# Setup moved into the first loop steps, and the residual's h added by an identity matmul

## The reference, cut to what matters

```python
h = layernorm(x) * (1 + ca) + sa
x = x + ga * attn(h)            # attn(h) = h + h_out @ W_out.T
h = layernorm(x) * (1 + cb) + sb
x = x + gb * ffn(h)             # 8 experts, top 4 of 8, clipped SwiGLU
```

## Time and profile before

| | us |
|---|---|
| median of 3 runs (lowest to highest) | 864.83 (863.77 to 866.02) |
| the profiled execution | 862.44 |
| its span, first to last instruction | 860.7 |
| what lies around the span | 1.7 |

### The profile page before, as it was taken

The page is one execution under the profiler, slowest core; times in us unless marked ns, Lnnn a source line. Parts: engine busy times, 40 slices in busy tenths (PEclk is TensorE's granted clock), DMA queues, the critical chain, the costliest instruction groups (busy, mean ns, idle before and its releaser), DMA issues.

```text
span 860.7 us, 11466 instructions
## 1 busy us (share of the span) xinstructions
PE 621.6 (72%) x2762; PEld 460.0 (53%) x2762; DVE 708.6 (82%) x1833; ACT 545.1 (63%) x1267; POOL 686.7 (80%) x731
## 2 busy tenths in 40 slices
PE   4743404597878787777869787877779695868886
PEld 3411102375666556555647556555646474757775
DVE  3452999999898998989998999989998999998431
ACT  3444323566767776768676776767676767556785
POOL 0498868798988998999988998989998888734454
PEclk9877756698897989999997999999979899789999
DMA  8008375555364546373553635553736455640000
GB/s 236 10 4 198 76 157 116 119 113 109 81 132 85 111 88 146 70 161 73 131 103 80 131 75 112 103 127 73 161 65 142 86 130 97 140 88 7 14 6 7
DMA packets 90659, 85.28 MB, mean 99 GB/s; under 512 B 42920, under 2 KB 87264, under 8 KB 88416
## 3 DMA queue, kind: packets, MB, share of 16 engines
q1 hardware_dynamic: 90592, 84.55, 46.3%
HBM read 44.66 MB, written 39.85 MB: 98 GB/s over the span
## 4 chain that ended last, share of the span: by engine, by line
POOL 51%; DVE 19%; issue 11%; PE 11%; ACT 4%; DMA 2%; SPq 1%; POOLq 0%; DVEq 0%; ACTq 0%
POOL ex L407 11%; POOL lg L414 8%; POOL fold L391 7%; DVE ps L852 6%; DVE prod L844 6%; POOL yacc L460 6%; POOL up L465 5%; PE ps L1156 4%; PE ps L1169 3%; DVE nmax L822 2%; POOL fold L394 2%; DVE act_t L918 2%; POOL ex L399 1%; PE ps L1143 1%; DMA gu_rows<-_L_ffn_gate_up_proj_dram 1%
## 5 line engine op out<-in xcount | busy, mean ns | idle before, releaser
L1156 PE MATMUL ps<-h2t,wgu 128*128 128x256 f32 x1024 | 279.4, 421 | 7.8 <-ACT up L622 7.8
L1156 PEld LDWEIGHTS ps<-h2t,wgu 128*128 128x128 f32 x1024 | 211.2, 213 | 60.1 <-issue 18.2
L844 DVE TENSOR_TENSOR prod<-gates,ps 64x272 f32<-64x272 f32 x512 | 215.6, 421 | 20.9 <-DMA gates<-gate_dram 14.4
L852 DVE TENSOR_REDUCE ps<-prod 64x16 f32<-64x272 f32 x512 | 219.6, 429 | 8.9
L1143 PE MATMUL ps<-wl,ht 128*128 128x512 f32 (+1 forms) x320 | 171.7, 644 | 68.6 <-ACT lg L605 65.0
L1169 PE MATMUL ps<-wd,act_t 128*128 128x128 f32 x1024 | 153.1, 297 | 50.3 <-DVE act_t L918 50.3
L1169 PEld LDWEIGHTS ps<-wd,act_t 128*128 128x128 f32 x1024 | 142.4, 209 | 71.8 <-DVE act_t L918 58.9
L414 POOL TENSOR_TENSOR lg<-lg,nmax 128x1088 f32<-128x1088 f32 x64 | 130.2, 2038 | 13.4 <-DVE nmax L822 11.8
L918 DVE SCALAR_TENSOR_TENSOR act_t<-ps,up 128x512 f32<-128x512 f32 x128 | 87.3, 682 | 58.1 <-ACT ps L628 48.1
L407 POOL TENSOR_TENSOR ex<-ex,rz 128x1088 f32<-128x1088 f32 x64 | 130.4, 2039 | 5.2 <-DVE rz L835 3.0
L465 POOL TENSOR_SCALAR up<-up 128x512 f32<-128x512 f32 x128 | 78.6, 614 | 66.7 <-ACT up L622 60.3
(11 more groups left out here) (122 smaller groups left out, 609.4 us busy)
## 6 DMA issues: line engine op xcount, KB each, us to landing
gate_dram<-ex SPq DMA_DIRECT2D x256, 136.0 KB, 3.0
gates<-gate_dram SPq DMA_DIRECT2D x32, 1088.0 KB, 8.3
yt_tok<-y_dram SPq DMA_DIRECT2D x256, 8.0 KB, 5.5
xg<-in_L_attn_x_dram SPq DMA_DIRECT2D x32, 64.0 KB
y_dram<-ys SPq DMA_DIRECT2D x32, 64.0 KB, 2.2
out_dram<-res_out SPq DMA_DIRECT2D x32, 64.0 KB
wa_rows<-in_L_attn_W_a_dram SPq DMA_DIRECT2D x1, 1088.0 KB, 8.2
dn_rows<-in_L_ffn_down_proj_dram SPq DMA_DIRECT2D x1, 1024.0 KB, 12.8
```

Source lines behind the costliest of these rows:

```text
L844: nc.vector.tensor_tensor(prod[:, :].rearrange("p (i k) -> p i k", k=M1), gates[:, t, :].rearrange("p (i k) -> p i k", k=M1), state[:, (t ...
L852: nc.vector.tensor_reduce(state[:, t % TS, 1:M1], prod[:, :].rearrange("p (i k) -> p i k", k=M1), AX_X, ALU.add).then_inc(scan.sem, 1)
L1156: last = nc.tensor.matmul(gu_ps(m, k, which)[:, q * N:(q + 1) * N], wgu[:, k, rows + q * P:rows + (q + 1) * P], h2t[:, m % 2, :], start=Tr ...
```

## The change

- `setup(it)` runs at the head of each loop step. PE, ACT and DVE handle the five WA groups at step 1 (into banks 0 to 4) and the 13 expert groups at step 3 (into banks 2, 3, 4, 7). Step 0 has only the first norm and h of chunk 0. `first_h` of chunk 0 waits for the six copies of the modulation vectors, no longer for the gate signs, which DVE now makes in `setup(1)`.
- SP's order of loads: c, wmod, x of chunk 0, gate weights, small weights, x of chunk 1, biases, experts' weights. The ring of x has six slots, freed by `xn_ok`.
- `res` is gone. `ht`, the transposed h, becomes a ring of five, and `project_y` adds `ht.T @ ident` in the bank of y's projection, so that `go = (y @ W_out + h) * ga`, and `new_residual` adds x itself.
- On SP the gate load of tile 0 stands ahead of the gate stores of tile 1, together with the store and load of y of tile 0.
- The written orders of GpSimd, ACT, PE and the slots u of DVE are changed. GpSimd has `finish` at the head of the step, `clamp_up` 3 behind `new_residual`, the root mean square's `inv_sqrt` between the two `sub_max` of tile 1, and `second_h` directly behind `clamp_up` 5. PE has `logits` 0 ahead of `gate_up` 0, `turn_h` after `logits` 9 and `down` 3, and `route` ahead of `gate_up` 7. ACT has the first normalise behind expert 1, and `h_out` and expert 6's activations ahead of `second_h_out`.

```diff
+    RX, RH, RN = 6, 5, 3
+            for it in range(NC + DEPTH - 1):
+                setup(it)
+                run(*[it - d if 0 <= it - d < NC else None for d in range(DEPTH)])
+        FREE_BANKS = (2, 3, 4, 7)
+        WA_AT, EXPERTS_AT = 1, 3
...
                 for j in range(TILES):
+                    if e is not None:
+                        store_gates(e, j)
                     if s is not None:
+                        store_y(s, j)
                     if e is not None:
+                        load_gates(e, j)
                     if s is not None:
+                        load_y(s, j)
...
                 if is_first(a):
-                    pool.wait_ge(mod_ready, 1)
+                    pool.wait_ge(mod_step, 6)
...
-            def residual(a):
-                if a >= RR:
-                    pool.wait_ge(xn_ok.sem, xn_ok.at(a - RR, 1))
-                pool.wait_ge(h_ok.sem, h_ok.at(a, 1))
-                nc.gpsimd.tensor_tensor(res[:, a % RR, :, :], hh[:, :, :], both(2), ALU.mult).then_inc(gh_ok.sem, 1)
-                pool.wait_ge(gh_ok.sem, gh_ok.at(a, 1))
-                nc.gpsimd.tensor_tensor(res[:, a % RR, :, :], res[:, a % RR, :, :], xg[:, a % RX, :, :], ALU.add
...
-                nc.gpsimd.tensor_tensor(xn[:, p % RN, :, :], go[:, :, :], res[:, p % RR, :, :], ALU.add
+                nc.gpsimd.tensor_tensor(xn[:, p % RN, :, :], go[:, :, :], xg[:, p % RX, :, :], ALU.add
...
             def run(a, g, e, s, p, m, o):          # GpSimd
+                if o is not None:
+                    finish(o)
                 if e is not None:
                     fold_row(e, 0)
                 if a is not None:
                     pool.wait_ge(mv1_ok.sem, mv1_ok.at(a, TILES))
                     inv_sqrt(mv1[:, :, 1], eps_mean, ve1, rs1, ve1_ok, rs1_ok, a)
-                if o is not None:
-                    finish(o)
...
+                if it == EXPERTS_AT:               # TensorE
+                    pe.wait_ge(in_gu, 16)
+                    pe.wait_ge(in_dn, 16)
+                    pe.wait_ge(in_gub, 16 * 3)
+                    for i in range(N_GROUPS - N_WA):
+                        bank = FREE_BANKS[i % 4]
...
-                    last = nc.tensor.matmul(bank_a(j), yt[:, j * P:(j + 1) * P], wo[:, :], start=True, stop=True)
+                    nc.tensor.matmul(bank_a(j), yt[:, j * P:(j + 1) * P], wo[:, :], start=True, stop=False)
+                    last = nc.tensor.matmul(bank_a(j), ht[:, p % RH, j * P:(j + 1) * P], ident[:, :], start=False,
+                                            stop=True)
...
+                if p is not None:
+                    route(p)
                 if m is not None:
+                    gate_up(m, 7)
```

More of the change, by code:

```diff
@@ new lines, in store_gates @@
+            def store_gates(e, j):
+                sp.wait_ge(norm_ok.sem, norm_ok.at(e, 2 * j + 2))
+                sp.sem_inc(passed_sp, 1)
+                if not is_first(e):
+                    sp.wait_ge(g_ld[j].sem, g_ld[j].at(e, 0))
+                    sp.sem_inc(passed_sp, 1)
+                for b in range(B):
+                    sp.dma_start(gate_dram[j, b].rearrange("r t e -> t r e"),
+                                 ex[b * TS:(b + 1) * TS, j, :].rearrange("p (r e) -> p r e", e=ROW)
+                                 ).then_inc(g_st[j].sem, 16)
@@ new lines, in load_y @@
+            def load_y(s, j):
+                sp.wait_ge(y_st[j].sem, y_st[j].at(s, 16))
+                sp.sem_inc(passed_sp, 1)
+                if not is_first(s):
+                    sp.wait_ge(yt_ps.sem, yt_ps.at(s - 1, 1))
+                    sp.sem_inc(passed_sp, 1)
+                for b in range(B):
+                    sp.dma_start(yt_tok[b * TS:(b + 1) * TS, j, :].rearrange("t (h i) -> t h i", h=H),
+                                 y_dram[j, b].rearrange("h t i -> t h i")).then_inc(y_ld[j].sem, 16)
@@ L314, in run @@
+            def run(a, g, e, s, p, m, o):
+                if a is not None and 1 <= a < NC - 1:
+                    if a + 1 >= RX:
+                        sp.wait_ge(xn_ok.sem, xn_ok.at(a + 1 - RX, 1))
+                        sp.sem_inc(passed_sp, 1)
+                    load_x(a + 1)
                 if o is not None:
@@ L356, in _ @@
+            whole(run, setup)
             for j in range(TILES):
@@ L514, in run @@
                     new_residual(p)
+                if m is not None:
+                    clamp_up(m, 3)
                 if g is not None:
@@ L524, in run @@
                 if m is not None:
-                    accumulate(m, 2)
+                    clamp_up(m, 5)
+                if p is not None:
+                    second_h(p)
+                if m is not None:
+                    accumulate(m, 3)
+                    accumulate(m, 4)
+                    clamp_up(m, 6)
+                    accumulate(m, 5)
+                if g is not None:
+                    sub_max(g, 1, 0)
                 if a is not None:
@@ L693, in run @@
                     up_and_silu(m, 0)
-                if a is not None:
-                    normalise(xh, xg[:, a % RX, :, :], rs1, nm1, nm1_ok, xh_ok, a)
                 if g is not None:
@@ L699, in run @@
                     up_and_silu(m, 1)
+                if a is not None:
+                    normalise(xh, xg[:, a % RX, :, :], rs1, nm1, nm1_ok, xh_ok, a)
                 if g is not None:
@@ L748, in run @@
                     router_exp(p)
-            whole(act, run)
+            whole(run, setup)
         @block.vector
@@ L1025, in between @@
                             aggregate(st2, mv2, st2_ok, mv2_ok, p, j)
-                elif u == 62:
-                    if m is not None:
-                        hidden(m, 4)
                 elif u == 63:
@@ L1032, in between @@
                 elif u == 64:
+                    if m is not None:
+                        hidden(m, 4)
                     if g is not None:
@@ L1228, in run @@
             def run(a, g, e, s, p, m, o):
+                if g is not None:
+                    logits(g, 0)
                 if m is not None:
@@ L1231, in run @@
                 if g is not None:
-                    logits(g, 0)
                     logits(g, 1)
+                if m is not None:
+                    gate_up(m, 1)
+                if g is not None:
                     logits(g, 2)
                 if m is not None:
-                    gate_up(m, 1)
                     turn_combine(m)
@@ L1239, in run @@
                     logits(g, 3)
+                    logits(g, 4)
                 if m is not None:
@@ L1242, in run @@
                     down_bias(m)
-                if g is not None:
-                    logits(g, 4)
-                if m is not None:
                     gate_up(m, 2)
                     down(m, 1)
+                if g is not None:
+                    logits(g, 5)
                 if p is not None:
@@ L1269, in run @@
                     down(m, 3)
+                if a is not None:
+                    turn_h(a, p)
+                if m is not None:
                     gate_up(m, 5)
```

420 lines of the change are left out of this document (190 added, 230 removed).

## The result

The changed kernel takes 812.95 us (median of 4 runs, 809.41 to 814.65) against 864.3 for the kernel before (median of 4 runs): a ratio of 0.9397, 95% interval 0.9361 to 0.9433. The forecast was 822, with a range of 807 to 843. Its profiled execution took 814.07, with a span of 812.3.

A forecast was written before the change was run, and what follows sets the result against it. DVE (44.1 us) and POOL (44.7), nearly full and waiting for each other, bound the full step. Gains 19.7 + 18 + 3.0 + 0.5 = 41.2 off 862.44 gave 821.2; 1 added, 822, range 807 to 843.

The forecast's parts named there:

- rival C: Full steps: all of DVE's waits vanish and the step is DVE's 44.1; 811 to 812 us, chance 0.10.
- The start: Before step 3: first logits at 18.3, scan at 64.3 instead of 84.05, 19.7 us earlier, bounds 14 to 21.
- SP's order: Start: tile 0's gate load needs only its own eight stores: 5.1, some 3 to land, 8.5 for the load.
- The 1.1 for `inv_sqrt`: Start: the root mean square's `inv_sqrt` behind the third `sub_max` no longer waits for the last logits, about 1.1 us.
- The experts' block: Step 3 on PE: the experts' 13 groups end between 58 and 62.5, hidden in DVE's wait for the gates.
- The full steps: Ten steps, 6 to 15: 45.1 us each, a gain of 1.8 a step, 18 in all; bounds 44.1 and 46.4.
- The wait before `second_h`: POOL in full steps: a new wait after the second norm's `inv_sqrt`, 1.3 us, bounds 0 and 2.
- `finish` at the head: POOL in full steps: `finish`, now first, waits for expert 7's weighted output, 0 to 0.6 us.
- rival D: Full steps: the wait of `finish` at POOL's head becomes DVE's too, +2.2 a step; 870 us, chance 0.03.
- half of its 1.49: Full steps: taking off POOL's two products, 1.49 us a step, would with the old order give perhaps half.
- The named cures: Full steps: reorders on PE and POOL shrink DVE's four waits of 14.6, 5.9, 4.0 and 3.2 us.
- The drain and step 5: Outside the full steps: 3.0 us from steps 5 and 16 to 18, 0.5 from steps 19 to 21.

The follow-up runs named there:

- Experiment 2: The changed kernel with the written orders of POOL, ACT, PE and DVE's slots as before; setup spread, SP order and residual stay changed: 847.12 us, ratio 0.9746.
- experiment 12: The changed kernel with SP storing the gates of both tiles before it loads tile 0, as before: 814.64 us, ratio 0.9411.
- experiment 6: The changed kernel with only POOL's written order as before, residual products still gone: 816.74 us, ratio 0.9426.
- experiment 7: The changed kernel with PE's `route` behind `gate_up` 7 again: 813.32 us, ratio 0.9398.
- experiment 1: The kernel before with only the residual changed (rings, identity matmul, POOL's two products gone), setup and orders as before: 869.3 us, ratio 1.0003.
- Experiment 4: The changed kernel with `finish` on POOL behind the first norm's `inv_sqrt` again, not at the head of the step: 809.58 us, ratio 0.9332.
- experiment 3: The changed kernel with POOL's two residual products put back behind `clamp_up` 2, their result unused: 836.15 us, ratio 0.9634.
- experiments 9 and 11: The changed kernel with only ACT's written order as before (825.11 us, ratio 0.9528), and with only DVE's slots as before (828.72 us, ratio 0.9569).
- experiment 5: The kernel before with only the residual changed, plus four filler matmuls on PE in its wait for `second_h`: 863.19 us, ratio 0.9979.

## Why the prediction was right, and where its steps failed

**The number.** 812.95 lies in the range, 9 below the forecast and 1 above the time of rival C (811 to 812). C's way there was that all of DVE's waits vanish and the step is DVE's 44.1. DVE's old waits did nearly vanish, but a new one of 0.87 came, and the rest of the step is 43.6: a step of 44.64 lies between the two. So the forecast's mechanism held in its parts, the start above all, and its time was nearer to a rival's.

**The start: right.** First logits at 17.82 (18.3 was said), scan at 63.14 (64.3), gain 20.9 (19.7). Experiment 2 shows it as a part of its own. SP's order came out as summed: from the end of `norm_gates` of tile 0 to the scan the sum has 5.1 + 3 + 8.5 = 16.6, where it took 19.2 before; the trace has 63.14 - 46.85 = 16.3. By experiment 12 the move is worth 3.4 there and 2.6 behind step 3. (The expectation of experiment 12, 4.5 to 5.5, left out that the load in the new order waits 2.6 for the eighth store to land, while in the old order it is issued 0.1 behind the sixteenth.) Of the two reorders, `gate_value` gave its 0.5: from the fold's start to the end of `norm_gates` it took 13.2, and 13.7 with POOL's old order (experiments 2 and 6) and before. The 1.1 for `inv_sqrt` can't be seen: the fold starts at 33.62, and at 33.63 and 33.19 with POOL's old order. The start as a whole varies by more, 63.14 here and 61.44 in experiment 7.

**The experts' block: hidden, as said.** It ran from 48.28 to 53.9 and DVE then waited 8.59 for the gates. The trace after:

```profile
41.73:48.28 6.55, 6.52 (x14) 3.12 (x15) 5.92 (x10) 4.12 (x11) 6.33 (x6) 0.76 0.06 10
48.28:54.00 5.72, 5.72 (x52) 5.35 (x50) 4.75 (x8) 4.47 (x10) 5.72 (x4) 1.00 0.88 179
```

The 32 transposes took 3.80, 0.12 each, at the upper level: PE had been busy with logits from 41.73 up to them, and its clock had risen within that stretch. (In experiment 1, where these transposes still stand ahead of the loop, they came every 0.21 while the granted clock was 0.50, from 20.3 to 23.0, and every 0.11 behind that at 1.00. So the 0.20 of the earlier trace rows is the lower level.) The prediction let the block start out of an idle time, which was not there. The rule of the Trainium skill ("TensorE: Matmul & The Clock Gate", part 1), that activity releases the clock, agrees with these two rows; its cold case did not occur.

**The full steps: the size was off.** Forecast 45.1, measured 44.64, 22.9 less in ten steps and not 18. Three terms were off:
- The wait before `second_h` was put at 1.3 and is 0.49.
- `finish` at the head was put at 0 to 0.6 on POOL, and is 0.55; that the fold behind it makes DVE wait 0.87 was foreseen only in rival D. Experiment 4 shows the two waits to be one stall: both go with the move. It is worth 3.4 us by the medians.
- DVE's own row came out at 44.64 - 1.05 = 43.6 and not 44.1. The short gaps that the list of waits leaves out are not the reason: step less waits less busy time is 1.1 in both kernels. DVE's busy time itself fell, from 42.98 to 42.46 a step, with the same 1131 instructions in ten steps. Why is open.

**"With the old order it would give perhaps half of its 1.49": wrong.** Removal and identity matmul together give nothing there (experiment 1). In the new order the removal gives 1.80 a step (experiment 3 against the result) and 2.4% of the whole. The other way round, the new orders are worth 34 us without the products (experiment 2 against the result); with them the kernel takes 836.15, 11 below experiment 2. So the value of each half depends on the other: without the orders the freed time turns into POOL's and DVE's waiting for ACT. One caveat stays, since experiment 3 leaves the identity matmuls in: how much of the nothing in experiment 1 is their cost was not separated.

**The named cures: one of them wrong.** The waits did nearly all go, as forecast. `logits` 0 ahead of `gate_up` 0 was named for the whole wait for silu, 14.6. Of that only 3.4 stood before `hidden` of expert 0; 9.0 stood before that of expert 2, in four waits, and 2.2 before that of expert 6. The move fits in part all the same: with PE's old order 6.4 is back, 2.3 for expert 0 and 4.1 for expert 2. POOL's order fits for its clamps (8.3 back in experiment 6), a gain that `finish` at the head hid. The wait for xn (3.2) went with the products: it is gone in experiment 1 with the old orders and back, 6.5, in experiment 3. But `route` had no part in it. And the prediction named no cure on ACT and little in DVE's slots, which cost 12 and 16 us when undone (experiments 9 and 11). What cured a wait was read from the diff, not from the trace.

**The drain and step 5.** 3.5 was forecast for steps 5 and 16 to 21, 5.4 came. Together with 1.2 in the start and 4.9 in the full steps, less 0.8 in step 3, that is the 7.2 by which the span fell further than 41.2. The rest of the difference to 822 is the step from the profiled execution to the median, put at +1 and measured at -1.1. Rivals A, B, D and E did not occur; C came half true, as said above.

## What to carry to other kernels

When two engines are both nearly full and wait for each other, taking work off one of them may give nothing at all and, in another order, more than the work itself: time the removal in both orders before judging it. Name each order's move with the wait that it is to cure, and undo them one engine at a time, then parts of one engine's order: an order that seems to give nothing may hold a good move and a bad one, as POOL's did here. Setup that fitted into a wait for DMA cost nothing here and was worth about its whole length, since the first step's latency shifts all that follows.

## What the runs showed of the hardware

Where TensorE's clock is low decides more than how low it is on average. In the changed kernel a step of 44.9 (mean granted clock 0.91) begins in a stretch at the lower level and one of 44.0 (0.96) does not. In the kernel before, steps took 45.7 at 0.96 and 47.6 at 0.86. But in experiment 6 the short steps include those with the lowest mean, 43.79 at 0.89, and the long ones, 45.5, have 0.95.

Behind an idle time of 1.97 us (after others in the same step) PE was granted 0.50 and a group of eight matmuls took 3.45 in place of 1.89. The runs of experiment 1, one kernel, span 857.6 at 0.879 to 869.5 at 0.841: time and clock go together, and which is the cause is not shown by that. What keeping PE busy in its wait gives was too small or too variable to be shown in the medians (experiment 5).

The identity matmul was not timed by itself. DVE has no wait for its result in the full steps of the changed kernel or of experiment 1, but it stands in PE's row, and experiments 1 and 5 time it together with the removal.
